# Expert stages as one sequence over both groups with the quads side by side, and a token-MLP stage without GpSimd

## The chip, the cores and the metric

The kernel runs on one NeuronCore of one Trainium2 chip. The metric is the device time of one execution in microseconds (us); lower is better. Everything between the layers stays in SBUF, in one float32 tensor `T` of 128 partitions by 17 images (16 and one of padding) by 25 token tiles by 32 channels. An image has 56x56 = 3136 tokens, that is 24 tiles of 128 and one of 64.

## The reference

For an input x of shape 16x56x56x32, float32:

```
x = x + window_attention(group_norm(x))                    # stage 1
x = LN4(y + mlp_b(y)),  y = LN3(LN2(z + mlp_a(z)) + bo_recv),  z = LN1(x + bo_time)   # stage 2
for layer in (L2, L3):
    t = t + causal_attention(layernorm(t))                 # per image, 3136 tokens
    t = t + expert_choice(layernorm(t))

LNi(v)   = (v - mean) * rsqrt(var + 1e-5) * g_i + be_i     # over 32 channels
mlp(v)   = gelu(v @ W1 + b1) @ W2 + b2                     # 32 -> 128 -> 32

expert_choice(x):                                          # 16 experts, 8 tokens each, per image
    logits = x @ gate_w.T + gate_b                         # 3136 x 16
    probs  = softmax(logits, over tokens); keep the 8 largest per expert
    pooled[e] = sum over kept tokens of prob * x[token]    # 32 numbers
    out[e] = [gelu([pooled, 1] @ weight1[e]), 1] @ weight2[e]
    y[token] += prob[token, e] * out[e]
```

## The kernel before

`program` runs seven stages one after the other, each in blocks with a barrier of all engines at its end: `window_attention`, `token_mlps`, then twice `causal_attention` and `expert_choice`, then the stores. The change touches `token_mlps` (L611 on) and `expert_choice` (L1545 on).

**token_mlps.** The 16 images are four quads q of 4 images, each a tensor `X[q]` of 128x3200. A quad goes through norm 1, MLP a, norm 2, norm 3, MLP b, norm 4. TensorE and ScalarE run 56 steps g (2 MLPs x 4 quads x 7 spans of 512 tokens, the last span 64): flip to channels (L854, copied at L912), four hidden matmuls with a Gelu each (L866, L918), the second matmul (L878, read at L925) and the flip back (L889, L932). Each engine's order is written out by hand. VectorE walks the list `LNS`: a "centre" is a sum over channels, a scaling and a subtraction (L807 to L809); a "scale" is the sum of the squares, fourteen short steps of an inverse root and a product with the whole quad (L819 to L823). GpSimd adds `bo_time` (L735), squares the quad for 14 of the 16 scales (L728), and multiplies by g2 and adds be2 (L745, L747), then g4 and be4 (L752 to L756). The first and the last square are ScalarE's (L907, L954), and the last quad's g4 and be4 VectorE's (L830 to L833). `results(q, i)` counts the steps done when a quad has its MLP's result. Two buffers `SQ` hold squares, so square n waits until scale n-2 has summed its own.

**expert_choice.** A first block loads the weights and waits for all of them (15 DMAs, L1634 to L1639). Then a hardware loop (`nc.Fori`, L1656) runs twice, for a group of 8 images that is two quads h, with a barrier at the end of each turn. In a turn VectorE normalises both quads into `XN` (L1765, L1770). For one quad after the other TensorE flips the tokens (L1679, copied to `XT` at L1742) and then computes logits (L1686, read at L1744 into 64 partitions of `LG`). After both, VectorE finds the 8 largest (L1783), ScalarE takes the exponential (L1754), and VectorE marks the kept tokens (L1787, L1788). TensorE flips the weights (L1694, copied at L1750 and L1748) and pools the tokens (L1702), all tiles of quad 0 before those of quad 1; each float32 product is two instructions in the trace. The experts' two layers follow (L1711, Gelu at L1757, L1716) with short VectorE steps between (L1792 to L1805), and the results (L1726), which VectorE adds to `T` (L1813). Four PSUM banks form a ring for all fills.

Of the kernel before, what the change touches and what calls it, by code (L numbers as in the profile page):

```python
# [20 lines left out]
P = 128  # L21
# [589 lines left out]
def token_mlps(nc, m, k, w, eps, tag):  # L611
# [31 lines left out]
    FIRST, FINAL = (0, 1), (NQ - 1, 4)  # L643
    SQUARED = {x: n for n, x in enumerate(y for y in SCALED if y not in (FIRST, FINAL))}

    with ExitStack() as ctx:
# [34 lines left out]
        added, centred, scaled = sem("added"), sem("centred"), sem("scaled")  # L681
        squared, squared_act, sq_read, vec = sem("squared"), sem("squared_act"), sem("sq_read"), sem("vec")
        affine, grown, stored = sem("affine"), sem("grown"), sem("stored")
# [12 lines left out]
        with nc.Block() as block:  # L696
# [20 lines left out]

            @block.gpsimd
            def _(pool):
                def square(q, which):  # L720
                    if which in (1, 3):
                        pool.wait_ge(centred, CENTRED[q, which] + 1)
                    else:
                        pool.wait_ge(x_done, results(q, which // 2 - 1))
                    n = SCALED[q, which]
                    if n >= 2:
                        pool.wait_ge(sq_read, n - 1)
                    nc.gpsimd.tensor_tensor(SQ[n % 2][:], X[q][:], X[q][:], ALU.mult).then_inc(squared, 1)  # L728

                def row(name, n=NT, r=P):  # L730
                    return ROW[name][0:r, None, None, :].to_broadcast([r, n, QD, C])

                pool.wait_ge(time_in, 16)
                for q in range(NQ):
                    nc.gpsimd.tensor_tensor(X[q][:], images(q), row("bo_time"), ALU.add).then_inc(added, 1)  # L735
                    if q >= 2:
                        square(q - 1, 1)
                square(NQ - 1, 1)
                pool.wait_ge(w_ready, 2)
                for q in range(NQ):  # L740
                    square(q, 2)
                    if q:
                        square(q - 1, 3)
                    pool.wait_ge(scaled, SCALED[q, 2] + 1)
                    nc.gpsimd.tensor_tensor(X[q][:], X[q][:], row("g2"), ALU.mult).then_inc(grown, 1)  # L745
                    pool.wait_ge(grown, q + 1)
                    nc.gpsimd.tensor_tensor(X[q][:], X[q][:], row("be2"), ALU.add).then_inc(affine, 1)  # L747
                square(NQ - 1, 3)
                for q in range(NQ - 1):
                    square(q, 4)  # L750
                    pool.wait_ge(scaled, SCALED[q, 4] + 1)
                    nc.gpsimd.tensor_tensor(X[q][:], X[q][:], row("g4"), ALU.mult).then_inc(grown, 1)  # L752
                    pool.wait_ge(grown, NQ + q + 1)
                    nc.gpsimd.tensor_tensor(images(q)[:, 0:NT - 1], X[q][:, 0:NT - 1], row("be4", NT - 1),
                                            ALU.add).then_inc(stored, 1)
                    nc.gpsimd.tensor_tensor(images(q)[0:LAST, NT - 1:], X[q][0:LAST, NT - 1:], row("be4", 1, LAST),  # L756
                                            ALU.add).then_inc(stored, 1)
                pool.wait_ge(stored, 2 * NQ - 2)

            @block.vector  # L760
            def _(dve):
# [36 lines left out]

                for kind, q, which in LNS:
                    x = X[q][:].rearrange("p t b c -> p (t b) c")  # L800
                    if kind == "centre":
                        n = CENTRED[q, which]
                        if which == 1:
                            dve.wait_ge(added, q + 1)
                        else:
                            dve.wait_ge(affine, q + 1)
# [4 lines left out]
                        dve.wait_ge(centred, n + 1)  # L811
                    else:
                        n = SCALED[q, which]
                        sq = SQ[n % 2][:].rearrange("p t b c -> p (t b) c")
                        if (q, which) in SQUARED:
                            dve.wait_ge(squared, SQUARED[q, which] + 1)
                        else:
                            dve.wait_ge(squared_act, 1 if (q, which) == FIRST else 2)
                        nc.vector.tensor_reduce(VAR[:], sq, AX.X, ALU.add).then_inc(sq_read, 1)  # L819
# [6 lines left out]
                        if (q, which) == FIRST:  # L826
                            weights()
                        if (q, which) == FINAL:
                            row = [ROW[n][:, None, None, :].to_broadcast([P, NT, QD, C]) for n in ("g4", "be4")]
                            step(nc.vector.tensor_tensor(X[q][:], X[q][:], row[0], ALU.mult))  # L830
                            step(nc.vector.tensor_tensor(images(q)[:, 0:NT - 1], X[q][:, 0:NT - 1], row[1][:, 0:NT - 1],
                                                         ALU.add))
                            step(nc.vector.tensor_tensor(images(q)[0:LAST, NT - 1:], X[q][0:LAST, NT - 1:],  # L833
                                                         row[1][0:LAST, NT - 1:], ALU.add))
# [69 lines left out]
            def _(act):  # L904
                nc.scalar.preload_act_table(ACT.Gelu)
                act.wait_ge(centred, CENTRED[FIRST] + 1)
                nc.scalar.activation(SQ[SCALED[FIRST] % 2][:], X[0][:], ACT.Square).then_inc(squared_act, 1)  # L907
# [28 lines left out]

                take_flip(0)
# [14 lines left out]
                act.wait_ge(x_done, NG)  # L952
                act.wait_ge(sq_read, SCALED[FINAL] - 1)
                nc.scalar.activation(SQ[SCALED[FINAL] % 2][:], X[NQ - 1][:], ACT.Square).then_inc(squared_act, 1)  # L954
# [590 lines left out]
def expert_choice(nc, m, k, gate_wT, gate_b, weight1, weight2, tag):  # L1545

# [9 lines left out]
    NO = m.NB // NI  # L1556
    QB = 512
    CH = -(-S // QB)
    TB = QB // P
    NB4 = -(-NT // TB)  # L1560
# [4 lines left out]
    def span(f):  # L1565
        return QB * f, min(QB * (f + 1), S)

    with ExitStack() as ctx:
# [9 lines left out]
        XN = sb("xn", [P, NT, NI, C])  # L1578
        XT = sb("xT", [P, S])
        LG = sb("lg", [P, S])  # L1580
        EX = sb("ex", [P, S])
# [7 lines left out]
        M8 = sb("m8", [P, TOPK])  # L1589
        NM = sb("nm", [P, 1])  # L1590
        SUM = sb("sum", [P, 1])
        RS = sb("rs", [P, 1])
        PM = sb("pm", [P, QD, C])
        PL = sb("pl", [P, C])
        PN = sb("pn", [P, C])
# [3 lines left out]
        OB = sb("ob", [P, C])  # L1599
# [3 lines left out]
        PP = pb("pp", [P, QD * C])  # L1603
        SM = [pb(f"sm{i}", [P, P]) for i in range(3)]

        w_in, w_set = sem("w_in"), sem("w_set")
        with nc.Block() as block:
            @block.vector
            def _(dve):
                nc.vector.memset(GW[:], 0.0).then_inc(w_set, 1)  # L1610
                nc.vector.memset(PT[:], 1.0).then_inc(w_set, 1)
                dve.wait_ge(w_set, 2)

            @block.gpsimd
            def _(pool):

                s1, s2 = sem("s1"), sem("s2")
                nc.gpsimd.memset(SAME[:], 1.0).then_inc(s1, 1)
                pool.wait_ge(s1, 1)
                n = 1  # L1620
                for h in range(NH):
                    part = SAME[h * 64:(h + 1) * 64]
                    for sign, base in ((1, 0), (-1, E_ - 1)):
                        nc.gpsimd.affine_select(out=part, in_=part, compare_op=ALU.is_ge, fill=0.0, base=base,
                                                pattern=[[-sign * E_, QD], [0, C]],
                                                channel_multiplier=sign).then_inc(s1, 1)
                        n += 1
                        pool.wait_ge(s1, n)

            @block.sync  # L1630
            def _(sp):
                sp.wait_ge(w_set, 1)
                for b in range(QD):
                    sp.dma_start(GW[b * C:(b + 1) * C, b * E_:(b + 1) * E_], gate_wT).then_inc(w_in, 16)  # L1634
                for b in range(NI):
                    sp.dma_start(GB[b * E_:(b + 1) * E_, :], gate_b[:, None]).then_inc(w_in, 16)
# [3 lines left out]
                sp.wait_ge(w_in, 16 * (QD + NI + 3))  # L1640

        norm_step = sem("norm_step")
        ring_full, ring_read_a, ring_read_v = sem("ring_full"), sem("ring_read_a"), sem("ring_read_v")
        vec, exp_done = sem("vec"), sem("exp_done")
        pooled_done, small_full, gelu_done = sem("pooled_done"), sem("small_full"), sem("gelu_done")


# [8 lines left out]
        with nc.Fori(0, NO) as o:  # L1656
            with nc.Block() as block:
# [75 lines left out]
                def _(act):  # L1733
                    for n in range(N_A):
# [4 lines left out]
                        if x == "xT":  # L1739
                            if h and f == 0:  # L1740
                                pass
# [162 lines left out]
```

## Time and profile before

| | us |
|---|---|
| runs shown, median (lowest to highest) | 5225.98 (5218.76 to 5230.42) |
| profiled execution, its own time | 5203.04 |
| its span, first to last instruction | 5201.3 |
| token_mlps, 1281 to 1691 of the span | 410 |
| first expert stage, 3227.7 to 3424.5 | 196.8 |
| second expert stage, 4962 to 5160 | 198 |

Times of instructions are read from the profiled execution. PE is TensorE (PEld its weight loads), DVE is VectorE, ACT is ScalarE, POOL is GpSimd. PEclk is the granted TensorE clock as a share of 2.4 GHz, so 0.50 is 1.2 GHz. In brackets behind a row stands how long the engine had been idle and what released it.

### The profile page before, as it was taken

The numbers are of one execution on the slowest core, as the hardware profiler recorded it, in microseconds if no ns is written. First come the engines' busy times: TensorE is split into PE (matmuls) and PEld (weight loads), VectorE is DVE, ScalarE is ACT, GpSimd is POOL, SyncE is SP. The second block draws the span as 40 slices with busy tenths as digits, with TensorE's granted clock in tenths as the row PEclk, the third lists the DMA queues.
The fourth block names the chain that finished last, engine by engine and source line by source line (L and its number), as shares of the span: only waits on it lengthen the run. The fifth ranks groups of instructions, "written<-read, shape, count | busy, mean of one in ns | idle before, by whom it ended". The sixth has DMA issues, their size and how long they took to land. (4 is left out here: it accounts for less than half of the span.)

```text
span 5201.3 us, 102304 instructions
## 1 busy us (share of the span) xinstructions
PE 4473.6 (86%) x39002; PEld 2775.7 (53%) x39002; DVE 3218.9 (62%) x6562; ACT 2836.1 (55%) x5790; POOL 1475.1 (28%) x2257
## 2 busy tenths in 40 slices
PE   4888888886754899999999997679999999999955
PEld 2666666665322455555555554555555555555544
DVE  4777777776796466666666564336666666666532
ACT  2766676665654356555555554315555555655521
POOL 3111111111354333334243322023333243333100
PEclk8998999988877799999999998769999999999966
DMA  1100000000000000000000000000000000000003
GB/s 26 27 2 2 2 2 2 2 2 3 1 1 0 1 2 2 2 2 2 2 2 2 2 2 5 1 1 2 2 2 2 2 2 2 2 2 2 2 5 49
DMA packets 348174, 22.44 MB, mean 4 GB/s; under 512 B 346388, under 2 KB 347700, under 8 KB 347700
## 3 DMA queue, kind: packets, MB, share of 16 engines
q1 hardware_dynamic: 347700, 16.03, 4.2%
q8 instruction: 308, 5.05, 0.4%
q14 instruction: 166, 1.36, 0.1%
HBM read 7.88 MB, written 6.42 MB: 3 GB/s over the span
## 5 line engine op out<-in xcount | busy, mean ns | idle before, releaser
L551 DVE TENSOR_REDUCE L2a_mx<-L2a_r 128x1 f32<-128x512 f32 (+4 forms) x1344 | 771.0, 627 | 334.2 <-PE L2a_r L415 326.8
L551 DVE TENSOR_REDUCE L3a_mx<-L3a_r 128x1 f32<-128x512 f32 (+4 forms) x1344 | 770.8, 627 | 331.3 <-PE L3a_r L415 323.7
L415 PE MATMUL L2a_r<-L2a_vT,L2a_qT 32*128 32x512 f32 (+3 forms) x3488 | 885.5, 529 | 13.2 <-DVE L2a_mx L551 12.5
L415 PE MATMUL L3a_r<-L3a_vT,L3a_qT 32*128 32x512 f32 (+3 forms) x3488 | 881.8, 527 | 12.9 <-DVE L3a_mx L551 12.3
L514 ACT ACTIVATE L2a_e<-L2a_r 128x512 f32<-128x512 f32 (+3 forms) x1344 | 669.1, 569 | 266.8 <-PE L2a_r L394 263.3
L514 ACT ACTIVATE L3a_e<-L3a_r 128x512 f32<-128x512 f32 (+3 forms) x1344 | 669.0, 569 | 266.7 <-PE L3a_r L394 263.2
L394 PE MATMUL L2a_r<-L2a_qT,L2a_vT 32*128 32x512 f32 (+4 forms) x3488 | 772.4, 513 | 2.8 <-DMA L2a_qT<-L2a_nm 2.7
L394 PE MATMUL L3a_r<-L3a_qT,L3a_vT 32*128 32x512 f32 (+4 forms) x3488 | 770.8, 511 | 3.8 <-DMA L3a_qT<-L3a_nm 3.8
L415 PEld LDWEIGHTS L2a_r<-L2a_vT,L2a_qT 32*128 32x128 f32 x3488 | 387.4, 190 | 158.5 <-DVE L2a_mx L551 90.1
L415 PEld LDWEIGHTS L3a_r<-L3a_vT,L3a_qT 32*128 32x128 f32 x3488 | 385.8, 189 | 156.7 <-DVE L3a_mx L551 89.8
L1471 POOL TENSOR_SCALAR win_xw<-win_xr,win_rs,win_sh 32x343 f32<-32x343 f32 (+7 forms) x432 | 186.5, 446 | 937.0 <-DVE win_sh L1340 936.9
L394 PEld LDWEIGHTS L3a_r<-L3a_qT,L3a_vT 32*128 32x128 f32 x3488 | 352.9, 187 | 128.8 <-issue 73.1
L394 PEld LDWEIGHTS L2a_r<-L2a_qT,L2a_vT 32*128 32x128 f32 x3488 | 352.5, 186 | 128.2 <-issue 73.6
L487 PE MATMUL L3a_acc<-L3a_e,L3a_v 128*32 128x512 f32 (+4 forms) x3680 | 355.9, 467 | 3.8 <-issue 2.9
L487 PE MATMUL L2a_acc<-L2a_e,L2a_v 128*32 128x512 f32 (+4 forms) x3680 | 354.2, 466 | 3.9 <-issue 3.0
L1115 PE MATMUL win_sl<-win_mq,win_xw 113*64 113x196 f32 x2048 | 213.7, 353 | 101.2 <-issue 67.3
L1229 ACT COPY win_mq<-win_pq 32x392 f32<-32x392 f32 x512 | 246.5, 481 | 93.7 <-PE win_pk L1108 87.9
L357 POOL TENSOR_SCALAR_AFFINE_SELECT L2a_e<-L2a_e 128x128 f32<-128x128 f32 (+2 forms) x304 | 99.4, 328 | 609.3 <-ACT L2a_e L514 597.0
L357 POOL TENSOR_SCALAR_AFFINE_SELECT L3a_e<-L3a_e 128x128 f32<-128x128 f32 (+2 forms) x304 | 99.4, 327 | 609.1 <-ACT L3a_e L514 596.9
L1268 ACT COPY win_yb<-win_yp 64x512 f32<-64x512 f32 x256 | 148.5, 580 | 204.3 <-PE win_yp L1197 202.8
L487 PEld LDWEIGHTS L3a_acc<-L3a_e,L3a_v 128*32 128x32 f32 x3680 | 119.3, 111 | 229.9 <-issue 128.9
L487 PEld LDWEIGHTS L2a_acc<-L2a_e,L2a_v 128*32 128x32 f32 x3680 | 118.3, 111 | 229.7 <-issue 129.2
(376 smaller groups left out, 7573.8 us busy)
## 6 DMA issues: line engine op xcount, KB each, us to landing
L2a_qT<-L2a_nm SPq DMA_DIRECT2D x768, 0.5 KB, 2.0
L3a_qT<-L3a_nm SPq DMA_DIRECT2D x768, 0.5 KB, 2.0
T<-in_x SPq DMA_DIRECT2D x16, 384.0 KB, 3.8
out<-T SPq DMA_DIRECT2D x16, 384.0 KB, 4.0
win_mq<-win_nmt SPq DMA_DIRECT2D x256, 3.1 KB, 1.7
win_msk<-in_L_conv_pos_emb SPq DMA_DIRECT2D x49, 0.2 KB
L2a_qT<-L2a_nm SPq DMA_DIRECT2D x32, 0.2 KB, 1.8
L3a_qT<-L3a_nm SPq DMA_DIRECT2D x32, 0.2 KB, 1.8
```

The source lines that it names most:

```text
L357: nc.gpsimd.affine_select(out=e, in_=e, compare_op=ALU.is_ge, fill=0.0, base=0, pattern=pattern, channel_multiplier=-1).then_inc(mask_done, 1)
L394: last = nc.tensor.matmul(bank_of(x)[0:r, o:o + c1 - c0], VT[g0:g0 + C, img % 2, u * P:u * P + r], QT_[g0:g0 + C, img % 2, j * QB + c0:j * ...
L415: return nc.tensor.matmul(bank_of(x)[:, o:o + c1 - c0], QT_[g0:g0 + C, img % 2, q0:q0 + P], VT[g0:g0 + C, img % 2, c0:c1], start=start, st ...
L487: last = nc.tensor.matmul(ACC[cg:cg + C, a:b], V[0:r, img % 2, u, :], E[0:r, n % RE, o + a - c0:o + b - c0], start=start, stop=stop)
L514: nc.scalar.activation(E[0:r, n % RE, 0:w], bank_of(x)[0:r, 0:w], ACT.Exp).then_inc(exp_done, 1)
L551: return nc.vector.tensor_reduce(to, frm, AX.X, ALU.max)
L1115: last = nc.tensor.matmul(bank[half * SLOT:(half + 1) * SLOT, c0:c0 + HK], window(n, 2 * p + half), buf[:, slot, half, p].rearrange("p h c ...
L1229: last = nc.scalar.copy(MQ[0:C, q_slot(n), :, :, h, :], PQ[h * C:(h + 1) * C, 0:NW * K].rearrange("p (w f c) -> p f w c", f=2, c=K))
L1268: last = nc.scalar.copy(YB[r, n % 2, :, :, half, :].rearrange("p a h c -> p (a h) c"), YP[r, :].rearrange("p (a c) -> p a c", c=C))
L1471: last = nc.gpsimd.tensor_scalar(dst, s, RS[:], SH[:], ALU.mult, ALU.add)
```

## The change

**In token_mlps** GpSimd's block is gone. All 16 squares are ScalarE activations (`square`), put behind given steps of its sequence by the table `SQUARES`; -1 is ahead of the first flip. The `bo_time` add is a step "add" of `LNS` on VectorE, and the affine steps g2, be2, g4 and be4 are VectorE instructions right behind their scale.

**In expert_choice** the loop is gone: both groups are written out as one sequence in one block with the loads, with `XN`, `LG`, `EX` and the small vectors held twice. Waits on the weights stand where they are used. The normalisation runs in halves of the tiles. The flips of both quads of a span come one after the other, their logits share one bank and one ScalarE read, and in pooling and results the quads alternate tile by tile. The second group's front runs beside the first group's selection.

```diff
 # token_mlps
-    LNS = [("centre", 0, 1), ("scale", 0, 1)]
-    LNS += [("centre", q, 1) for q in range(1, NQ)]
+    LNS = [("add", 0, 1), ("centre", 0, 1), ("add", 1, 1), ("scale", 0, 1)]
     for q in range(1, NQ):
-        LNS.insert(LNS.index(("centre", q, 1)) + (2 if q + 1 < NQ else 1), ("scale", q, 1))
+        LNS += [("centre", q, 1)] + ([("add", q + 1, 1)] if q + 1 < NQ else []) + [("scale", q, 1)]
...
+    SQUARES = {(0, 1): -1, (1, 1): 2, (2, 1): 8, (3, 1): 13, (0, 2): 14, (1, 2): 18, (0, 3): 23, (2, 2): 25,
+               (1, 3): 31, (3, 2): 32, (2, 3): 38, (3, 3): 45, (0, 4): 46, (1, 4): 47, (2, 4): 53, (3, 4): NG + 2}
...
-            @block.gpsimd
...
+                    if kind == "add":
+                        step(nc.vector.tensor_tensor(X[q][:], images(q), row("bo_time"), ALU.add))
...
+                        elif which == 2:
+                            step(nc.vector.tensor_tensor(X[q][:], X[q][:], row("g2"), ALU.mult))
+                            step(nc.vector.tensor_tensor(X[q][:], X[q][:], row("be2"), ALU.add))
+                        elif which == 4:
+                            step(nc.vector.tensor_tensor(X[q][:], X[q][:], row("g4"), ALU.mult))
...
+                    if n >= 2:
+                        act.wait_ge(sq_read, n - 1)
+                    nc.scalar.activation(SQ[n % 2][:], X[q][:], ACT.Square).then_inc(squared, 1)
...
+                    for x, at in SQUARES.items():
+                        if at == g:
+                            square(*x)
 # expert_choice, VectorE
-        with nc.Fori(0, NO) as o:
...
+                normalise(0, 0)
+                normalise(0, 1)
+                normalise(1, 0)
+                maxima(0)
+                normalise(1, 1)
+                pick(0)
+                maxima(1)
+                pick(1)
+                take_pooled(0)
+                take_turned(0)
+                take_pooled(1)
+                take_second(0)
+                take_turned(1)
+                results(0)
+                take_second(1)
+                results(1)
 # expert_choice, TensorE
+                front(0)
+                front(1)
+                turn_weights(0)
+                pool_tokens(0)
+                turn_weights(1)
+                first_layer(0)
+                pool_tokens(1)
+                second_layer(0)
+                first_layer(1)
+                out(0)
+                second_layer(1)
+                out(1)
...
+                def pool_tokens(g):
...
+                        for t in tiles(f):
+                            for h in range(NH):
+                                last = nc.tensor.matmul(PP[64 * h:64 * h + 64, g], WT[0:r, t, 64 * h:64 * h + 64],
...
+                def out(g):
...
+                        for t in tiles(f):
+                            for h, x in enumerate(pair):
+                                ins = nc.tensor.matmul(bank_of(x)[0:r, c0:c0 + P],
+                                                       EX[g][64 * h:64 * h + 64, t * P:t * P + r],
 # expert_choice, ScalarE: xT, lg and wT reads in the order of the fills
+                    if x == ("lg", 1, 0, 1):
+                        exponential(0)
+                    if x == ("wT", 0, 0, NF - 1):
+                        exponential(1)
+                gelu(0)
+                gelu(1)
```

## Rows read from the trace of the kernel before

**Rows 1.** Windows, one for each stage: us, then busy us, PEclk, DMA share, GB/s.

```profile
1281.00:1691.00 410.00, 231.97 (x1416) 100.90 (x1416) 320.46 (x323) 207.50 (x395) 202.48 (x35) 0.77 0.01 1
1691.00:3227.70 1536.70, 1484.65 (x12200) 840.87 (x12200) 907.49 (x1803) 860.81 (x1793) 522.36 (x864) 0.96 0.04 2
3227.70:3424.50 196.80, 130.75 (x738) 109.51 (x738) 71.29 (x66) 49.06 (x80) 1.44 (x5) 0.68 0.02 3
4962.00:5160.00 198.00, 131.22 (x738) 110.36 (x738) 71.30 (x66) 49.28 (x80) 1.43 (x5) 0.67 0.02 3
```

**Rows 2.** Groups by line in token_mlps: busy us, mean ns, idle before, releasers.

```profile
L819 DVE TENSOR_REDUCE mlp_var<-mlp_sq 128x100 f32<-128x3200 f32 x16 | 55.8, 3486 | 54.3 <-POOL mlp_sq L728 51.0 <-ACT mlp_sq L907 3.0
...
L599 DVE TENSOR_SCALAR mlp_rt<-mlp_var 128x100 int32<-128x100 int32 x16 | 30.2, 1886 | 0.5
```

**Rows 3.** Timeline of GpSimd, then VectorE, in token_mlps: start, us, instruction.

```profile
1283.62 20.73 POOL L735 TENSOR_TENSOR mlp_x<-T,mlp_row_bo_time 128x3200 f32<-128x3200 f32 x3 [109.13 <-DMA mlp_row_bo_time<-in_L_conv_bo_time]
...
1326.81 0.16 DVE L794 COPY mlp_bbb<-mlp_u 128x1 f32<-128x1 f32 x1
...
1363.16 3.49 DVE L819 TENSOR_REDUCE mlp_var<-mlp_sq 128x100 f32<-128x3200 f32 x1
...
1374.35 3.49 DVE L807 TENSOR_REDUCE mlp_mean<-mlp_x 128x100 f32<-128x3200 f32 x1
1378.12 3.49 DVE L809 TENSOR_TENSOR mlp_x<-mlp_x,mlp_mean 128x3200 f32<-128x3200 f32 x1
...
1683.04 3.49 DVE L830 TENSOR_TENSOR mlp_x<-mlp_x,mlp_row_g 128x3200 f32<-128x3200 f32 x1
...
1689.96 0.28 DVE L833 TENSOR_TENSOR T<-mlp_x,mlp_row_be 64x128 f32<-64x128 f32 x1
```

**Rows 4.** Timeline of ScalarE in token_mlps.

```profile
1307.73 2.87 ACT L907 ACTIVATE mlp_sq<-mlp_x 128x3200 f32<-128x3200 f32 x1 [25.71 <-DVE mlp_x L809]
...
1343.48 0.71 ACT L925 ACTIVATE mlp_z<-mlp_u,mlp_bba 128x512 f32<-128x512 f32 x1
...
1397.57 1.27 ACT L918 ACTIVATE mlp_hs<-mlp_h,mlp_b1a 128x512 f32<-128x512 f32 x2 [1.40 <-PE mlp_h L866]
...
1425.11 1.27 ACT L918 ACTIVATE mlp_hs<-mlp_h,mlp_b1a 128x512 f32<-128x512 f32 x2 [1.40 <-PE mlp_h L866]
...
1480.23 1.27 ACT L918 ACTIVATE mlp_hs<-mlp_h,mlp_b1b 128x512 f32<-128x512 f32 x2 [2.75 <-PE mlp_h L866]
```

**Rows 5.** Timeline of VectorE in the first expert stage.

```profile
3239.77 3.49 DVE L1765 TENSOR_TENSOR L2f_xn<-T,mean 128x3200 f32 x1 [11.71 <-PEq L1607]
...
3266.07 3.43 DVE L1783 MAX8 L2f_m<-L2f_lg 128x8 f32<-128x3136 f32 x1 [12.17 <-ACT L2f_lg L1744]
```

**Rows 6.** Chain that ended last, in the second expert stage: start, us, what.

```profile
5108.89 5.03 PE L3f_r L1694 x24
...
5114.73 11.57 PE L3f_pp L1702 x100
...
5128.36 5.09 PE L3f_sm L1711 x32
...
5133.80 1.89 PE L3f_sm L1716 x32
...
5137.17 22.38 PE L3f_r L1726 x100
```

**Rows 7.** Groups by line and shape in the first expert stage.

```profile
L1744 ACT ACTIVATE L2f_lg<-L2f_r,L2f_gb 64x512 f32<-64x512 f32 x24 | 16.4, 682 | 5.2 <-PE L2f_r L1686 5.2
L1742 ACT COPY L2f_xT<-L2f_r 128x512 f32<-128x512 f32 x24 | 12.7, 588 | 16.4 <-PE L2f_r L1679 16.4
```

**Rows 8.** One window inside the result products (L1726), columns as in Rows 1.

```profile
3308.30:3319.50 11.20, 11.20 (x51) 10.64 (x51) 3.92 (x6) 0.00 (x0) 0.00 (x0) 0.50 0.00 1
```

**Rows 9.** Timeline of TensorE in the first attention: two row groups, then four column groups.

```profile
2502.51 0.19 PEld L394 LDWEIGHTS L2a_r<-L2a_qT,L2a_vT 32*128 32x128 f32 x2 [0.24 <-issue]
...
2505.39 1.90 PE L487 MATMUL L2a_acc<-L2a_e,L2a_v 128*32 128x512 f32 x16
```

More of the change, by code:

```diff
@@ L716, in _ @@
                 assert n == LOADS
-            @block.gpsimd
[L719 to L758, printed above, removed]
             @block.vector
@@ L935, in take_out @@
                     ins.then_inc(x_done, 1)
+                square(0, 1)
                 take_flip(0)
@@ L1588, in expert_choice @@
         SAME = sb("same", [P, QD, C])
[L1589 to L1592, printed above, removed]
+        M8 = [sb(f"m8{g}", [P, TOPK]) for g in range(NG)]
+        NM, SUM, RS = [[sb(f"{n}{g}", [P, 1]) for g in range(NG)] for n in ("nm", "sum", "rs")]
         PM = sb("pm", [P, QD, C])
-        PL = sb("pl", [P, C])
-        PN = sb("pn", [P, C])
+        PL, PN, OB = [sb(n, [P, C]) for n in ("pl", "pn", "ob")]
         PT = sb("pT", [C + 1, E_, NI])
@@ L1649, in expert_choice @@
[L1649 to L1677 removed]
+                sp.wait_ge(w_in, 48)
@@ new lines, in _, with bank_free, front @@
+            @block.tensor
+            def _(pe):
+                def bank_free(x):
+                    n = PLACE[x]
+                    if n >= RING:
+                        old = FILLS[n - RING]
+                        if old in BY_ACT:
+                            pe.wait_ge(act_read, BY_ACT[old] + 1)
+                        else:
+                            pe.wait_ge(dve_read, BY_DVE[old] + 1)
+                def front(g):
+                    for x in FILLS:
+                        if x[0] == "xT" and x[1] == g:
+                            _, _, h, f = x
+                            bank_free(x)
+                            pe.wait_ge(norm_step, 2 * (2 * g + (1 if tiles(f)[0] >= HALVES[1][0] else 0)) + 2)
+                            for t in tiles(f):
@@ new lines, in front @@
+                            last.then_inc(ring_full, 1)
+                        elif x[0] == "lg" and x[1] == g:
+                            f = x[3]
+                            lo, hi = span(f)
+                            bank_free(x)
+                            pe.wait_ge(gate_in, 16 * QD)
+                            for h in range(NH):
+                                pe.wait_ge(act_read, BY_ACT[("xT", g, h, f)] + 1)
+                                last = nc.tensor.matmul(bank_of(x)[64 * h:64 * h + 64, 0:hi - lo], GW[:],
+                                                        XT[h][f % RX][:, 0:hi - lo], start=True, stop=True)
+                            last.then_inc(ring_full, 1)
@@ new lines, in turn_weights @@
+                def turn_weights(g):
+                    pe.wait_ge(picked, g + 1)
+                    for f in range(NF):
+                        x = ("wT", g, 0, f)
+                        bank_free(x)
+                        for t in tiles(f):
+                            c0, r = (t % TB) * P, rows(t)
+                            last = nc.tensor.transpose(bank_of(x)[0:r, c0:c0 + P], EX[g][:, t * P:t * P + r], k.ident[:])
+                        last.then_inc(ring_full, 1)
+                def pool_tokens(g):
+                    for f in range(NF):
+                        pe.wait_ge(act_read, BY_ACT[("wT", g, 0, f)] + 1)
+                        for t in tiles(f):
+                            r = rows(t)
+                            for h in range(NH):
+                                last = nc.tensor.matmul(PP[64 * h:64 * h + 64, g], WT[0:r, t, 64 * h:64 * h + 64],
+                                                        XN[g][0:r, t, QD * h:QD * (h + 1)].rearrange("p b c -> p (b c)"),
+                                                        start=(t == 0), stop=(t == NT - 1))
+                    last.then_inc(pooled, 1)
@@ new lines, in first_layer @@
+                def first_layer(g):
+                    pe.wait_ge(mean_ready, g + 1)
+                    if g:
+                        pe.wait_ge(ok_ready, g)
+                    nc.tensor.transpose(SM[0][0:C, g], PN[:], k.ident[:]).then_inc(turned, 1)
+                    pe.wait_ge(w_in, 48)
+                    pe.wait_ge(pt_ready, g + 1)
+                    for e in range(E_):
+                        last = nc.tensor.matmul(SM[1][:, g, e * NI:(e + 1) * NI], W1[:, e, :], PT[:, e, :],
+                                                start=True, stop=True)
+                    last.then_inc(hidden, 1)
@@ new lines, in second_layer @@
+                def second_layer(g):
+                    pe.wait_ge(gelu_done, g + 1)
+                    for e in range(E_):
+                        last = nc.tensor.matmul(SM[2][0:C, g, e * NI:(e + 1) * NI], W2[:, e, :],
+                                                HT[:, e * NI:(e + 1) * NI], start=True, stop=True)
+                    last.then_inc(second, 1)
+                    pe.wait_ge(ot_ready, g + 1)
+                    nc.tensor.transpose(SM[0][:, g, 0:C], OT[:].rearrange("o b e -> o (b e)"),
+                                        k.ident[0:C, 0:C]).then_inc(ot_turned, 1)
@@ new lines, in out @@
+                def out(g):
+                    pe.wait_ge(ok_ready, g + 1)
+                    for f in range(NF):
+                        pair = [("out", g, h, f) for h in range(NH)]
+                        for x in pair:
+                            bank_free(x)
+                        for t in tiles(f):
+                            c0, r = (t % TB) * P, rows(t)
+                            for h, x in enumerate(pair):
+                                ins = nc.tensor.matmul(bank_of(x)[0:r, c0:c0 + P],
+                                                       EX[g][64 * h:64 * h + 64, t * P:t * P + r],
+                                                       OK[64 * h:64 * h + 64].rearrange("p b c -> p (b c)"),
+                                                       start=True, stop=True)
+                                if t == tiles(f)[-1]:
+                                    ins.then_inc(ring_full, 1)
```

367 lines of the change are left out of this document (155 added, 212 removed).

## Prediction

> **What bounds the kernel now.** I read the windows by stage first. Two of the stages that the change touches have no engine that is busy all the time: token_mlps takes 410 us with VectorE busy for 320.5, TensorE for 232.0 and ScalarE for 207.5; an expert stage takes 196.8 and 198.0 us with TensorE busy for 131 and VectorE for 71 [rows 1]. These are chains of waits, while the attention stages are TensorE's (1484.65 of 1536.7 us) and no line of them changes. Then the groups by line: in token_mlps VectorE waits 54.3 us ahead of the sum of squares, 51.0 of it for GpSimd's square [rows 2]. It is also slow there: the inverse root's first step has a mean of 1886 ns [rows 2], though a whole scale, fourteen such steps included, took 11.19 us (1363.16 to 1374.35) where GpSimd stood idle [rows 3]. Last the chain that ended last: in the expert stages it passes from engine to engine with nothing beside it [rows 6].
>
> **token_mlps: VectorE's new work.** I price every step by the rows without GpSimd beside them. A scale is 11.19 us, 16 of them 179.0. A centre is from 1374.35 to the end of the subtraction, 1378.12 + 3.49 = 1381.61, so 7.26, 8 of them 58.1. The four bo_time adds, new on VectorE, are a two-operand pass over 3200 elements as L830: 3.52 with its gap, 14.1. The g2/be2 pair is two of these, 7.05, four times 28.2. The g4/be4 pair ran from 1683.04 to 1690.24 = 7.2 on the last quad; four times 28.8 [rows 3]. What finishes the weights (short instructions and a wait for TensorE) ends at 1326.97 [rows 3]; the first square ended at 1310.6 [rows 4], its scale 11.2 later, so it takes 5.1 us. Sum 313.3 us. Against the 320.5 busy before, that is 64 us of work taken over (14.1 + 28.2 + 21.6) and some 71 us of stretched instructions gone.
>
> The stage can't be shorter than this, so I walk the waits. VectorE's first add starts where GpSimd's started, at 1283.6, when bo_time lands [rows 3]. ScalarE's square takes 2.87 us; seven steps g of ScalarE take 1425.11 - 1397.57 = 27.54 us, 3.96 for a full one; with 16 squares ScalarE has 8 x 27.54 + 46 = 266 us of work, less than VectorE [rows 4].
> - The weights are ready at 1314.1 instead of 1326.97. Square (1,1) stands behind step 2, which ended at 1344.2 before, 17.2 us after the weights [rows 3, 4]; now 1331.3, and 2.9 for the square: 1334.3. VectorE has done centre (1,1) and add 2 at 1325.0: 9.3 us of waiting.
> - Squares (2,1) and (3,1), behind steps 8 and 13, come at 1360.7 and 1383.2; VectorE waits 4.4 and 4.1.
> - From 1383 on VectorE is behind by its affine steps, and each square is ready before its scale: (0,2) at 1390, (1,2) at 1409, (0,3) at 1431, all used later. Now TensorE's flip of a quad for MLP b waits for VectorE, in steps 27, 34 and 41; each time ScalarE idles and needs a restart (2.75 us idle in the old one [rows 4]).
> - Scale (2,3) ends at 1522.8. Quad 2's steps start again at 1528.8, and square (3,3) stands behind step 45, four full steps later: 1547.5. VectorE is through centre (3,3) at 1530.1: 17.4 us, the largest wait.
> - From 1547.5 on nothing is late: (0,4), (1,4), (2,4) are ready at 1554, 1561, 1588 and the last at 1600, ahead of its scale at 1614.
>
> The waits add to 35.2 us. 1283.6 + 313.3 + 35.2 = 1632.1 against 1690.24: **58 us less**. ScalarE's squares lie under VectorE's work; without that cover they would cost up to 46 us. A wide step of VectorE was between 3.49 us and 10 us in this stage beside GpSimd; I take the lower end, since GpSimd is idle in the whole stage now. At worst the 71 us of stretch stay.
>
> On this the Trainium skill says, in "SBUF — State Buffer", section "Who interferes with whom", that a two-input instruction of VectorE blocks against a GpSimd one that reads SBUF, for all its duration, and that a reduction never does. The trace agrees: the reduction L819 has a mean of 3486 ns over all 16, undisturbed [rows 2]. By that rule the whole stretch goes, as I sum it.
>
> **Expert stage: what goes.** VectorE's first normalisation waited 11.71 us for the loads [rows 5]; it now starts at 3228.1, behind two memsets. Until the gate weights are used there are 7 us of normalisation, and 50 us until W1 and W2 are. The idle time in the two turns goes as far as the other group's work covers it. I walk one stage, times as in the first one.
> - Normalising is 3.49 + 3.49 us for a quad [rows 5], 28.5 us for all four halves: the halves end at 3235.0, 3242.4, 3249.2, and the last, behind the maximum of group 0.
> - ScalarE's fills: per span two copies of 0.588 and one read of 0.682 [rows 7], now for both quads: 1.86 us, 2.6 with the gaps to TensorE; I take 2.2. Spans 3 to 6 follow the second half: logits of group 0 complete at 3250.3.
> - Maximum (3.43, [rows 5]) until 3253.9, last half until 3261.3. The exponential is done by 3258.7, so VectorE marks the tokens (3.4 + 3.4 us, a pass of the maximum's length each) until 3268.4.
> - Group 1's logits are complete at 3269.3, its maximum at 3272.9. Its exponential stands behind the reads of group 0's flipped weights (5.5 us, 5.03 in [rows 6]): 3274.9 to 3278.0. Marked at 3285.1.
> - Flip of group 1's weights until 3290.4; first layer of group 0 (5.09 [rows 6]) and its Gelu until 3296.8; pooling of group 1; second layer of group 0 (1.89 [rows 6]) and four short steps until 3306.4; first layer of group 1 until 3312.5; results of group 0; 3.4 us of second layer and short steps; results of group 1.
>
> Two prices in it are new. **Results.** Before, 100 instructions took 22.38 us [rows 6], 220 ns each at a granted clock of 0.50 (1.2 GHz) though TensorE never paused [rows 8]. With the quads alternating they use two row groups. The attention runs such pairs: two weight loads in different row groups in 0.19 us together [rows 9]. Bounds: nothing gained, 22.4; both the pairing and 2.4 GHz, 5.6, and then VectorE's 12 adds of 0.69 bound it at about 9.5. I take the pairing alone, at the clock of the nearest row: 10.7 plus a last add. **Pooling.** 100 instructions took 11.57 us, 116 ns each [rows 6]; alternating they use two column groups. In the attention 16 instructions of 512 columns, on four column groups, took 1.90 us, 119 ns each [rows 9], where 220 ns for 128 columns at half clock make 440 for 512 at the full one: 3.7 times faster. Bounds 5.8 and 11.6; I take 6.2.
>
> Against pooling the Trainium skill has a rule, in "TensorE: Matmul & The Clock Gate", section "The mechanism": weight loads overlap running matmuls only where the row groups differ, and these pairs share their rows. By that alone pooling keeps its 11.6 us; group 1's is on the path, and a stage is 5.4 us longer, two of them 11. The column groups above speak against it.
>
> So the stage ends at 3312.5 + 10.7 + 3.4 + 10.7 + 0.7 = 3338.0 instead of 3424.4: 86 us less, and 173 us in both. The loop's end (about 1 us) and its barrier are in that.
>
> **Sum.** 58 + 173 = 231 us. The profiled execution took 5203.0, so the changed one 4972. The runs shown have their median 23 us higher, at 5226; I carry this over: **4995 us**.
>
> **Rivals.**
> - *Row and column groups don't overlap* with two instructions of one quad in a row. Results then 22.4 twice (+23.4), pooling of group 1 +5.4: 58 us in two stages, 5053. For it: the pair order is new for shapes of 64 rows. Against: the rows of the attention.
> - *ScalarE's order stalls the MLPs.* It serves its queue in order: a square whose centre is late holds every Gelu behind it, TensorE runs dry, and the next square is later still. The stage gains nothing if the waits are 93 us, not 35: 5053. Three squares in the first quads have under 4 us in hand.
> - *The change doesn't do what it says: VectorE stays slow without GpSimd.* The stretch of 71 us stays: 5066. Against: [rows 3] shows it gone wherever GpSimd is idle.
> - *The results run at 2.4 GHz and VectorE bounds them:* 1.2 us less each, and up to 6 us less in the small layers of a stage: about 4983. Within my own range.
> - *Slower: the attention pays.* It is TensorE's for 2970 us of both stages at a granted 0.96 [rows 1]. If the busier stages ahead of it brought this down, each 0.01 costs 32 us; the gain is used up from 0.96 / (1 + 231 / 3074) = 0.893 on; at 0.88 it is 280 us: 5275. Against: 1500 us of nearly unbroken work don't lower it now.
>
> **How the numbers follow.** Forecast 0.77 (the 2.4 GHz case in it), no overlap 0.08, ScalarE's order 0.07 and 0.02 more for waits that eat the whole gain (35 + 231 = 266 us, ScalarE's whole work laid end to end with VectorE's), slow VectorE 0.04, slower 0.02. The walk is good to 8 us for each expert stage and 15 for token_mlps, so the likeliest case alone spans 4965 to 5025. 8 in 10 is 4950 to 5058, with part of the two cases at 5053. What a measurement can tell from no change is 0.2%, 10 us: faster 0.96, same 0.02, slower 0.02.
>
> **What would show it.** Right: token_mlps near 351 us, L599 at 0.21 us, the longest wait of VectorE ahead of square (3,3); an expert stage near 110 us, pooling near 6 us and results near 11 at a granted 0.50. Wrong: an attention stage that moves by over 5 us, results still at 220 ns an instruction, or more than 60 us of waits ahead of the sums of squares.

## Result and the profile after

The changed kernel takes 4984.69 us (median of 4 runs, 4968.6 to 4988.89) against 5222.56 us before (5218.76 to 5230.42): a ratio of 0.9549, 95% interval 0.9531 to 0.9566, 238 us less. The profiled execution had a span of 4983.4 us.

The windows by stage, columns as in [rows 1]. token_mlps is first, then attention, experts, attention, experts.

```profile
1293.00:1643.90 350.90, 254.14 (x1416) 111.28 (x1416) 301.88 (x343) 245.07 (x409) 0.00 (x0) 0.83 0.01 1
1643.90:3181.40 1537.50, 1485.00 (x12200) 841.54 (x12200) 908.10 (x1805) 861.13 (x1793) 522.39 (x864) 0.96 0.05 2
3181.40:3290.10 108.70, 82.11 (x738) 65.30 (x738) 69.36 (x64) 35.99 (x63) 10.73 (x5) 0.79 0.04 6
3290.10:4834.00 1543.90, 1491.12 (x12200) 843.42 (x12200) 908.07 (x1805) 861.36 (x1793) 522.40 (x864) 0.96 0.04 2
4834.00:4942.50 108.50, 81.19 (x738) 64.77 (x738) 69.35 (x64) 35.86 (x63) 10.73 (x5) 0.80 0.04 6
```

Against [rows 1] token_mlps is 59 us shorter and the expert stages 88 and 90 us. The unchanged stages moved the other way: the window attention's part ahead of token_mlps was 12 us longer than before, the second attention 6 us. That is within what they do from profile to profile, whatever the kernel: over all the profiles here the first was between 1273 and 1295 us and an attention between 1533 and 1545 us, while a changed stage that was left alone repeated within 1.3 us. So a few us are read from a stage's own length, not from the total.

In token_mlps, the groups by line that answer to [rows 2]:

```profile
L774 DVE TENSOR_REDUCE mlp_var<-mlp_sq 128x100 f32<-128x3200 f32 x16 | 55.8, 3486 | 34.8 <-ACT mlp_sq L873 34.4
L768 DVE TENSOR_TENSOR mlp_x<-mlp_x,mlp_mean 128x3200 f32<-128x3200 f32 x8 | 27.9, 3492 | 0.3
L599 DVE TENSOR_SCALAR mlp_rt<-mlp_var 128x100 int32<-128x100 int32 x16 | 3.4, 212 | 0.6
```

L599 fell from 1886 to 212 ns: the stretch is gone. The waits for squares are 34.4 us in all. The timeline of VectorE has the four long ones, for (1,1), (2,1), (3,1) and (3,3):

```profile
1347.68 3.48 DVE L774 TENSOR_REDUCE mlp_var<-mlp_sq 128x100 f32<-128x3200 f32 x1 [10.47 <-ACT mlp_sq L873]
1373.33 3.49 DVE L774 TENSOR_REDUCE mlp_var<-mlp_sq 128x100 f32<-128x3200 f32 x1 [3.67 <-ACT mlp_sq L873]
1394.79 3.48 DVE L774 TENSOR_REDUCE mlp_var<-mlp_sq 128x100 f32<-128x3200 f32 x1 [3.00 <-ACT mlp_sq L873]
...
1558.96 3.49 DVE L774 TENSOR_REDUCE mlp_var<-mlp_sq 128x100 f32<-128x3200 f32 x1 [17.08 <-ACT mlp_sq L873]
```

In the first expert stage, the timeline of TensorE from the pooling of group 0 to the end (L1763 pooling, L1754 flip of the weights, L1776 first layer, L1799 results), and the windows of the two results:

```profile
3228.41 5.83 PE L1763 MATMUL L2f_pp<-L2f_xn,L2f_wT 128*64 128x128 f32 x100
...
3240.22 5.18 PE L1754 MATMUL L2f_r<-ident,L2f_ex 128*128 128x128 f32 x25 [5.98 <-DVE L2f_ex L1653]
...
3250.97 7.81 PE L1763 MATMUL L2f_pp<-L2f_xn,L2f_wT 128*64 128x128 f32 x100
...
3262.18 6.75 PE L1776 MATMUL L2f_sm<-L2f_pT,L2f_w 33*128 33x8 f32 x31 [0.56 <-DVE L2f_pT L1665]
...
3268.95 4.73 PE L1799 MATMUL L2f_r<-L2f_ok,L2f_ex 64*128 64x128 f32 x47
...
3285.92 2.36 PE L1799 MATMUL L2f_r<-L2f_ok,L2f_ex 64*128 64x128 f32 x32 [0.24 <-DVE T L1686]
```

```profile
3268.90:3278.20 9.30, 8.68 (x103) 7.70 (x102) 6.70 (x11) 0.28 (x1) 0.00 (x0) 0.83 0.00 0
3280.70:3289.00 8.30, 7.14 (x100) 6.08 (x100) 6.88 (x12) 0.00 (x0) 0.00 (x0) 1.00 0.01 2
```

The results take 9.3 and 8.3 us instead of 22.4, and TensorE waits for VectorE's adds in them: the granted clock, 0.50 before [rows 8], rises to 1.00. Two things are in this, and the start of the first results shows the one without the other. There the clock is still 0.50, and the product instructions (L1799 alone) come every 103 ns, against 220 ns in [rows 8] at the same clock:

```profile
3269.00:3272.10 3.10, 3.10 (x30) 3.10 (x30) 0.50 0.00 0
```

So the pairs overlap and take half the time; the higher clock comes on top.

Ahead of the results the clock was lower than in the pooling of group 0, which had 1.00. The windows are those of the first layer of group 0, of the pooling of group 1 right behind it, and of the first layer of group 1:

```profile
3246.10:3251.00 4.90, 4.90 (x34) 4.88 (x34) 0.00 (x0) 1.27 (x1) 0.00 (x0) 0.72 0.00 0
3251.00:3258.70 7.70, 7.70 (x101) 7.37 (x100) 0.00 (x0) 0.28 (x1) 0.00 (x0) 0.73 0.01 2
3262.20:3268.90 6.70, 6.70 (x33) 6.70 (x34) 0.00 (x0) 0.00 (x0) 0.00 (x0) 0.50 0.01 2
```

### The profile page after: what moved, and what is told of

Read it like the earlier page. It is cut to its first block and busy times, and to the rows that moved or that the text cites. A ratio compares the mean times of both kernels' runs of the same rounds, so it can differ in the third digit from the quotient of the medians.

```text
span 4983.4 us, 101485 instructions
## 1 busy us (share of the span) xinstructions
PE 4412.7 (89%) x39002; PEld 2705.1 (54%) x39002; DVE 3200.3 (64%) x6579; ACT 2848.2 (57%) x5770; POOL 1291.6 (26%) x2222
## 3 DMA queue, kind: packets, MB, share of 16 engines
q8 instruction: 313, 5.13, 0.4%
```

## Experiments

Ratios are to the kernel before, timed on the same chip as the experiment; "stage" is from a stage's first instruction to the next stage's.

**One half at a time.** Edits: the whole of `token_mlps`, or of `expert_choice`, taken from the kernel before.

> The expert stages of the changed kernel with the token_mlps of the kernel before. My theory: the two parts are independent and their gains add. In the traces token_mlps became 58.6 us shorter and the expert stages 88.4 and 88.9 us, so this kernel should take 5222.6 - 177 = 5046 us, with token_mlps at 409 us and expert stages at 108.5 us. Rival: part of the gain is the attention's (clock or placement), then an attention stage differs by more than 5 us from 1537 us and the total misses 5046 by more than 15 us.

> The token_mlps of the changed kernel with the expert stages of the kernel before. My theory: the gains add, so 5222.6 - 59 = 5164 us, token_mlps 351 us, expert stages 197 us each. Rival: the parts interact (GpSimd or the clock carry something from stage to stage), then this gain and the one of the other half don't sum to 238 us within 10 us.

Only the expert stages changed: 5039.26 against 5211.42 us, ratio 0.9661 (0.9629 to 0.9692), stages 108.9 and 108.2 us, token_mlps 409.8. Only token_mlps changed: 5157.77 us, 0.9895 (0.9868 to 0.9923), token_mlps 351.2, the first expert stage 196.3. The two gains are 3.4% and 1.05% and add to 4.4%, the whole change's 4.5%. In us they are 172 and 54, together 226, which misses the 238 by 12, more than the 10 that I had named as the mark of an interaction; but the runs of one of these kernels lie up to 29 us apart, so the totals can't settle it. The stages can: each has in the half kernels the length, within 1 us, that it has in the whole one or in the kernel before. The parts are independent.

**Alternation in the results.** First by span, then by whole quad.

```diff
 # e3_results_in_turn
-                        for t in tiles(f):
-                            for h, x in enumerate(pair):
+                        for h, x in enumerate(pair):
+                            for t in tiles(f):
 # e9_results_by_quad: fills, TensorE and VectorE
-                    for f in range(NF):
-                        for h in range(NH):
+                    for h in range(NH):
+                        for f in range(NF):
```

> The changed kernel, but in the result products the quads no longer alternate tile by tile: within a span the tiles of quad 0 come first, then those of quad 1. My theory: alternation lets two row groups of TensorE run at once, and with that the granted clock rises to 1.00 in this stretch (0.83 and 1.00 in the changed kernel, 0.50 before). Without it: 220 ns an instruction at 0.50, some 22 us for each group instead of 9.3 and 8.3, so 4 x 13 = 52 us more, 5037 us. Rival one: the clock is high because of what runs before it, not because of the pairs; then about 110 ns an instruction, 11 us a group, 8 us more in all, 4993 us. Rival two: the pairs overlap but the clock doesn't follow them: no such state has the clock at 0.50 here with fewer than 200 ns an instruction.

By span: 4982.36 us, stages 113.8 and 113.4, only 5 us more each. I was wrong that the order within a span decides. The windows of TensorE in the second stage's first results show why:

```profile
4914.70:4920.00 5.30, 5.30 (x40) 5.30 (x41) 2.20 (x4) 0.28 (x1) 0.00 (x0) 0.50 0.00 0
4920.00:4925.70 5.70, 5.70 (x65) 5.41 (x65) 5.15 (x9) 0.00 (x0) 0.00 (x0) 0.89 0.01 3
```

At 0.50 an instruction comes about every 132 ns, though one row group alone needs 220 [rows 8] and strict alternation 103: blocks of eight already overlap with the next block. "No state with fewer than 200 ns at 0.50" was false, and then the clock rises all the same.

> The changed kernel, but all result products of quad 0 come before those of quad 1 (fills, TensorE and VectorE alike), as in the kernel before. With blocks of eight instructions in turn 40 instructions took 5.3 us at a granted clock of 0.50 (132 ns each, less than the 213 of one row group), and then the clock rose. My theory now: TensorE runs ahead to the other row group over some instructions, so only a whole quad in one row group (56 instructions or so) is serial; the clock stays at 0.50 as long as one row group works alone. Then 22 us for each group as before, 13 us more four times: stages of 134 us, 4985 + 52 = 5037 us. Rival: the clock is set by what ran ahead (the first layer is as before, though), and rises here too: about 11 us a group, stages of 113 us, 4993 us.

5040.20 us, ratio to before 0.9650 (0.9615 to 0.9685), stages 135.7 and 136.1: 27 us more each, as forecast. One row of the timeline and the window of the second group:

```profile
4952.99 22.34 PE L1799 MATMUL L3f_r<-L3f_ok,L3f_ex 64*128 64x128 f32 x100
```

```profile
4978.60:5001.00 22.40, 22.34 (x100) 21.16 (x100) 8.40 (x14) 0.00 (x0) 0.00 (x0) 0.50 0.00 1
```

The work ahead of the first results is the same as in the changed kernel, so what ran before isn't the cause: a busy TensorE with one row group at work stayed at 1.2 GHz for 22 us, with two it went to 2.4. Whether it is the second row group that lifts the clock or the closer spacing of the instructions, no run separates. The alternation is worth 54 us of the 178.

**Alternation in the pooling**, the same two edits in `pool_tokens`.

> The changed kernel, but in the pooling the quads don't alternate: within a span quad 0's tiles come first, then quad 1's. My theory: two column groups of TensorE run at once only when the instructions alternate. Without it 116 ns an instruction as before, 11.6 us for group 0 instead of 5.8, and 12 to 14 us for group 1 instead of 7.8. Group 0's has 6 us in which TensorE waits afterwards, so it costs nothing; group 1's is on the path: 4 to 6 us for each stage, 8 to 12 us in all, 4995 us. Rival, the rule that weight loads overlap only where row groups differ: the alternation brought nothing, group 0's pooling stays at 5.8 us and the total at 4985 us.

> The changed kernel, but the whole pooling of quad 0 comes before that of quad 1, as in the kernel before. Blocks of eight in turn still overlapped: 6.9 and 8.6 us instead of 5.8 and 7.7. My theory: two column groups overlap, and by whole quads nothing can: 11.6 us for group 0, which eats the 6 us in which TensorE waited; 12 to 14 us for group 1, on the path: 5 us more for each stage, at most 1 us more from group 0, 4985 + 11 = 4996 us. Rival, from the rule that weight loads overlap only where row groups differ: no part of the gain in pooling is the alternation's and it stays at 5.8 us.

By span 4986.17 us in all, stages 112.4 and 111.9 us; pooling took 6.9 and 8.7 us. By quad 4978.77 us (0.9539, 0.9504 to 0.9573), stages 112.0 and 111.5 us, with this on TensorE in the second stage:

```profile
4869.51 11.56 PE L1763 MATMUL L3f_pp<-L3f_xn,L3f_wT 128*64 128x128 f32 x100
4881.32 2.95 PE L1754 MATMUL L3f_r<-ident,L3f_ex 128*128 128x128 f32 x25 [0.25 <-DVE L3f_ex L1653]
4884.94 3.71 PE L1776 MATMUL L3f_sm<-L3f_pT,L3f_w 33*128 33x8 f32 x32 [0.56 <-DVE L3f_pT L1665]
4888.57 13.22 PE L1763 MATMUL L3f_pp<-L3f_xn,L3f_wT 128*64 128x128 f32 x100
```

The column groups overlap: 5.83 against 11.56 us for group 0, at a granted clock of 1.00 in both. The Trainium skill's rule ("TensorE: Matmul & The Clock Gate", "The mechanism"), that weight loads overlap only where row groups differ, doesn't describe these pairs; the measurement decides. But a stage is only 3 us longer, not 5 (the total, 6 us below the changed kernel's, is too noisy to show it): with the slower pooling TensorE waits 0.25 us instead of 5.98 before the next flip, keeps its clock, and does flip and first layer in 2.95 and 3.71 us instead of the changed kernel's 5.01 and 5.13. The faster pooling had bought idle time and a lower clock behind it.

The run by span shows the same from the other side. There group 1's pooling is only 1.0 us longer (8.71 against 7.65 us in the second stage), but the stage 3.4 us. The windows of the two results in the second stage, first of the changed kernel, then of this run:

```profile
4921.20:4930.30 9.10, 8.49 (x102) 7.50 (x101) 6.66 (x11) 0.28 (x1) 0.00 (x0) 0.83 0.01 2
4932.80:4941.10 8.30, 7.14 (x100) 6.08 (x100) 6.84 (x12) 0.00 (x0) 0.00 (x0) 1.00 0.01 2
```

```profile
4920.60:4930.70 10.10, 9.28 (x102) 8.59 (x102) 6.89 (x12) 0.28 (x1) 0.00 (x0) 0.73 0.01 2
4933.20:4942.40 9.20, 8.59 (x100) 7.57 (x100) 6.68 (x11) 0.00 (x0) 0.00 (x0) 0.83 0.01 2
```

Results whose code is the same took 1.0 and 0.9 us more at a lower granted clock. So some 3 us a stage is what either edit costs, and a good part of it is the moment at which the clock falls or rises, not the pooling itself.

**The early start.** Edit: `dve.wait_ge(w_in, 48)` ahead of the first normalisation.

> The changed kernel with one wait more: VectorE's first normalisation in each expert stage waits for the last weight loads, as in the kernel before. My theory: the early start is worth what VectorE waited then, 11.7 us in each stage: stages of 120 us, 4985 + 23 = 5008 us. Rival: something later in the stage (the other loads, ScalarE) would hold the stage anyway and a part of the early start is lost: less than 8 us for each stage.

4995.72 us (5008 expected), stages 119.2 and 119.8: 10.5 and 11.3 us more. VectorE's wait for the loads was 11.00 and 11.41 us. By the stages the early start is worth nearly what was summed. With the results (54 us) and the pooling (6 us) it makes some 82 of the 178 us; the other 96 or so, from one group's work beside the other's, the shared logits reads and the loop's end, no run takes apart.

**GpSimd beside VectorE**, one execution each. Edit: in `token_mlps` a GpSimd block on two scratch tiles, in order by a semaphore: 40 times `tensor_tensor(G[1], G[0], G[0], mult)`, or 100 times `memset(G[i % 2], 1.0)`.

> The changed kernel with added work in token_mlps whose result nobody uses: GpSimd squares a scratch tile of 128x3200 forty times in a row, from the start of the stage. My theory: VectorE's stretch in the kernel before came from GpSimd's work itself, wherever its data lie. Then VectorE's products with two inputs and its short steps stretch here too while the sums (L774's line) stay at 3.49 us; 40 squares of 5.5 us cover 220 us, and at the rate of before (71 us of stretch beside 202 us of GpSimd) the stage is about 75 us longer, 4984 + 75 = 5060 us. Rival: the stretch came from both engines working on the same tiles X and SQ; then scratch data cost nothing and the stage stays at 351 us.

> The changed kernel with added work in token_mlps: GpSimd only writes, 100 memsets of a scratch tile of 128x3200 (some 2.5 to 5 us each). My theory, after the Trainium skill (SBUF — State Buffer, Who interferes with whom): an instruction of VectorE with two inputs is held up only by a GpSimd instruction that reads. Then the products with two inputs keep 3.49 us, and only the short one-input steps stretch, at most to the length of one memset: 10 to 60 us more in the stage. Rival: any GpSimd work blocks any VectorE instruction but a reduction; then the wide products stretch here as beside the squares.

Reading: 5180.07 us, stage 538.8, 187 us more. Writing: 5078.12 us, stage 455.2, 104 us more. The groups of the reading kernel, then of the writing one (L778, L776 and L602 are products of two inputs, L604 has one). They cover the whole stage, and so also the part after GpSimd's last instruction:

```profile
L778 DVE TENSOR_TENSOR mlp_x<-mlp_x,mlp_mean 128x3200 f32<-128x3200 f32 x8 | 38.6, 4830 | 0.3
L784 DVE TENSOR_REDUCE mlp_var<-mlp_sq 128x100 f32<-128x3200 f32 x16 | 55.8, 3486 | 27.2 <-ACT mlp_sq L883 26.8
...
L602 DVE TENSOR_TENSOR mlp_tm<-mlp_rt 128x100 f32<-128x100 f32 x48 | 39.2, 816 | 1.6
```

```profile
L776 DVE TENSOR_TENSOR mlp_x<-mlp_x,mlp_mean 128x3200 f32<-128x3200 f32 x8 | 27.9, 3492 | 0.3
L604 DVE TENSOR_SCALAR mlp_tm<-mlp_tm 128x100 f32<-128x100 f32 x48 | 47.7, 993 | 1.7
L602 DVE TENSOR_TENSOR mlp_tm<-mlp_rt 128x100 f32<-128x100 f32 x48 | 12.6, 262 | 1.6
```

The data were scratch, so it is the engine's work, not the shared tiles. Sums never stretched, two-input products only beside reads, one-input steps beside either. These kinds agree with the Trainium skill ("SBUF — State Buffer", "Who interferes with whom"): by it a reduction never contends, an instruction with two inputs contends only with a GpSimd instruction that reads, and a `tensor_scalar` can run in a mode that contends with GpSimd.

Both sizes were forecast far too low. The same groups, only while GpSimd is at work, first of the reading kernel (1299.5 to 1542 us), then of the writing one (1288.3 to 1570.5), show why:

```profile
L602 DVE TENSOR_TENSOR mlp_tm<-mlp_rt 128x100 f32<-128x100 f32 x5 | 27.9, 5582 | 0.2
L604 DVE TENSOR_SCALAR mlp_tm<-mlp_tm 128x100 f32<-128x100 f32 x5 | 27.6, 5512 | 0.2
```

```profile
L604 DVE TENSOR_SCALAR mlp_tm<-mlp_tm 128x100 f32<-128x100 f32 x21 | 42.0, 1998 | 0.7
L602 DVE TENSOR_TENSOR mlp_tm<-mlp_rt 128x100 f32<-128x100 f32 x21 | 5.5, 262 | 0.7
```

A step of 0.21 or 0.26 us waits for the end of a GpSimd instruction that is over ten times as long (5.99 and 2.77 us): in the trace each stretched step of the roots ends 0.06 to 0.12 us after one of them. In the kernel before, of the root's steps only the first two met GpSimd, and not in every root; L602 kept its 262 ns, and 202 us of GpSimd's work cost some 71. Forty squares without a break, 243 us, cost 187, since nearly every step met one; the memsets, 282 us, cost 104, about in the old proportion.

**More out of token_mlps.** e7 moves the squares (1,1), (2,1), (3,1), (3,3) to steps 1, 7, 12, 42. e8 adds a shorter root, in token_mlps alone; e11 has it with (2,1) and (3,1) at 6 and 11 and (0,4) at 43 and (1,4) at 46.

```diff
-        step(nc.vector.tensor_tensor(t, y, y, ALU.mult))
+        step(nc.vector.scalar_tensor_tensor(out=t, in0=y, scalar=-0.5, in1=y, op0=ALU.mult, op1=ALU.mult))
         step(nc.vector.tensor_tensor(t, t, v, ALU.mult))
-        step(nc.vector.tensor_scalar(t, t, -0.5, 1.5, ALU.mult, ALU.add))
-        step(nc.vector.tensor_tensor(y, y, t, ALU.mult))
+        step(nc.vector.scalar_tensor_tensor(out=y, in0=t, scalar=1.5, in1=y, op0=ALU.add, op1=ALU.mult))
```

> The changed kernel with four squares earlier in ScalarE's sequence: (1,1) behind step 1 instead of 2, (2,1) 7 instead of 8, (3,1) 12 instead of 13, (3,3) 42 instead of 45. In the changed kernel VectorE waits 10.5, 3.7, 3.0 and 17.1 us for them. My theory: the stage is VectorE's work plus these waits; (3,3) then comes 12 us sooner and (1,1) 4 us sooner, each of the other two saves at most what is left of its wait: 15 to 20 us less, about 4967 us. Rival: an earlier square holds the Gelus behind it until its centre is done, TensorE restarts later and the next square comes later by as much: less than 5 us gained.

> As the kernel with the four earlier squares, and the inverse root in token_mlps in 11 steps instead of 14: each of its three rounds has three instructions, not four, with the same operations. My theory: VectorE sets the stage, so 16 scales x 3 steps x 0.25 us = 12 us less again, about 4955 us. Rival: with VectorE shorter ScalarE's squares are late by as much and the waits take it back: no change against the kernel with the four earlier squares. If both hold in part, a two-input step in the place of a one-input one costs 0.05 us more and 10 us are left.

> The kernel with the 11-step inverse root, and the squares at steps 1, 6, 11 for (1,1), (2,1), (3,1), 42 for (3,3), 43 for (0,4) and 46 for (1,4). Moving (3,3) alone took its wait from 17.1 to 5 us but the next one, (0,4), then came 7.2 and 10.7 us late. My theory: with both early the waits fall from 31 to about 15 us, and then the last square, which ScalarE reaches some 310 us after its start, bounds the stage: 328 us, 7 us less than the 335.8 of the kernel with the 11 steps, 23 less than the changed kernel's 351: 4955 to 4962 us. Rival: ScalarE and TensorE are late by as much again and the stage stays within 2 us of 335.8.

The stage was 345.7, 335.8 and 333.1 us instead of 351.4, the medians 4965.97, 4961.53 and 4965.03 us. Moving squares gave 6 us in the stage, not 15 to 20, and e7's total is near the 4967 forecast by chance: the waits fell only from 34.4 to 28.9 us. In e7's timeline the wait for (3,1) rose from 3.00 to 6.93 us; the one for (3,3) is 5.34 us, and the next, for (0,4), now 7.20:

```profile
1548.86 3.49 DVE L774 TENSOR_REDUCE mlp_var<-mlp_sq 128x100 f32<-128x3200 f32 x1 [5.34 <-ACT mlp_sq L873]
1567.22 3.49 DVE L774 TENSOR_REDUCE mlp_var<-mlp_sq 128x100 f32<-128x3200 f32 x1 [7.20 <-ACT mlp_sq L873]
```

The shorter root gave 9.9 us of 10 to 12. e11's stage is 3 us shorter than e8's, not 7: its waits are still 27.9 us, where 15 were expected. Against the kernel before, e8's ratio is 0.9498 (0.9477 to 0.9518), below the changed kernel's interval; e11's is 0.9514 (0.9481 to 0.9548) and overlaps with both. So e8 is a faster version than both kernels; e11's stage is the shortest, and its total can't be told from e8's.

## Why the prediction was right, step by step

- **Total.** 4995 forecast, 4985 measured. The gains by stage were 58 and 173 forecast, 59 and 178 measured. The 23 us carried over stood for the unchanged stages, which were short in the profiled execution of before: right in kind, since they were some 19 us longer in the one after. Of the 10 us between forecast and result 7 are the larger gain, and 3 that the median before, timed beside the changed kernel, was 5222.56 and not 5226.
- **A sign of being wrong that was met.** I had named an attention stage that moves by over 5 us, and the second one moved by 6. The sign was too tight: over all the profiles an attention stage spans 12 us, in kernels that leave it alone, so it says nothing of the change.
- **VectorE's work in token_mlps** was priced at 313.3 us, gaps between its steps included. From the first add (1295.90) to the last step (1643.84) are 347.9 us, less 34.4 of waits 313.5, of which some 301 are busy. The undisturbed rows were the right ones.
- **The waits** were 35.2 forecast, 34.4 measured: (1,1) 9.3 against 10.5, (2,1) 4.4 against 3.7, (3,1) 4.1 against 3.0, (3,3) 17.4 against 17.1.
- **The expert stage's walk** gave 110.3 us, measured 108.7. Group 0 was marked 40.7 us after the start (40.9), group 1 57.4 (58.8). It hides two errors, in the next two points; that they nearly cancel is luck.
- **Results** were mis-sized: I took the pairing and left the clock at 0.50, 11.4 us with the last add; it was 9.3 and 8.3 us, VectorE-bound, as in the rival at 2.4 GHz. The halving by the pairs at 0.50 was right (103 ns an instruction); what was missing is that the clock then rises. That rival had the small layers faster too, which they were not.
- **Pooling of group 1 and the first layer of group 1** were mis-sized the other way: 6.2 and 5.1 us taken, 7.8 and 6.8 measured. I priced both by rows at a higher clock than the 0.73 and 0.50 that they had; I had reckoned with 0.50 in the results alone. These 3.3 us and the last point's error nearly cancel.
- **The rivals.** Without overlap in results and pooling I gave 58 us more, 47 and 11; measured one at a time, 54 and 6 us. The case didn't happen, and its price was right in the sum more than in the parts. ScalarE's order, a slow VectorE and a slower attention didn't happen.

## What to carry to other kernels

A gap of waits between stages can be priced by walking each engine's list with undisturbed durations. Where a matrix product uses half the rows or columns of TensorE, put two in different groups near each other, by blocks of eight instructions or alternating: here it overlapped them and, for row groups, the clock rose as well. It pays where the product is on the path: 54 us for the results, hardly more than the moves of the clock for the pooling. Keep GpSimd away from a chain of short VectorE steps, since each may wait for a whole GpSimd instruction.

## What was not expected of the hardware

- TensorE, without a pause, stayed at a granted 0.50 for 22.4 us with one row group of 64. With two, in blocks of eight, it had 0.50 for 5.3 us and a mean of 0.89 in the next 5.7.
- Overlap of groups needs no strict alternation: blocks of eight instructions gave about 132 ns at 1.2 GHz, strict alternation 103, one row group 220.
- GpSimd is held up too: four masks of `L2f_same` took 1.43 us before and 10.73 us beside VectorE's normalisation. They are first read at 3240.27, 48 us after the last of them, so it cost nothing. The row before, and after:

```profile
3228.02 1.43 POOL L1624 TENSOR_SCALAR_AFFINE_SELECT L2f_same<-L2f_same 64x128 f32<-64x128 f32 x4
3181.73 10.73 POOL L1606 TENSOR_SCALAR_AFFINE_SELECT L2f_same<-L2f_same 64x128 f32<-64x128 f32 x4
```
